# Passes over edges written out pair by pair, gather indices from one table in SBUF

## What is computed

```python
# layer 0: two convolutions with edge features (32), maximum over incoming edges
msg = x[src] @ W_msg + edge_attr_32 @ W_edge
agg = segment_max(msg, dst)                       # -inf -> 0
c   = leaky_relu(agg + x @ W_root + b)            # twice: c1, c2
# layer 1: edge features (17) through a small network, times the source's features, sum
w   = relu(edge_attr_17 @ W1.T + b1) @ W2.T + b2
agg = segment_sum(w * x[src], dst)
y   = relu(x @ Ws.T + bs + agg @ Wn.T + bn)
# layer 2: two hops h = segment_sum(norm[:, None] * h[src], dst), norm from the degrees
# layer 3: segment_sum((x * outdeg**-0.5)[src], dst) @ weight * indeg**-0.5 + bias
# after each layer: x = layernorm(x + layer(x))
```

## Time and profile before

| | before |
|---|---|
| median of three runs | 5490.79 us |
| the profiled execution | 5478.03 us, span 5476.3 us |
| granted TensorE clock, mean | 0.782 |
| PE / PEld busy | 73% / 48% |
| DVE busy | 41% |
| ACT busy | 18% |
| POOL busy | 47% |
| DMA, mean | 127 GB/s |

### The profile page before, as it was taken

One profiled execution on the slowest core, in us unless ns is written; L12 is line 12 of the kernel. 1 busy time (PEld: TensorE's weight loads), 2 busy tenths in 40 slices (PEclk: granted clock), 3 DMA queues, 4 the chain that ended last, 5 costly groups with the idle time before them and its releaser, 6 DMA issues.

```text
span 5476.3 us, 68119 instructions
## 1 busy us (share of the span) xinstructions
PE 3970.6 (73%) x19316; PEld 2615.8 (48%) x19316; DVE 2233.3 (41%) x5877; ACT 998.9 (18%) x2108; POOL 2583.1 (47%) x2689
## 2 busy tenths in 40 slices
PE   5766666676556667676746777766768668999999
PEld 4333333333423333333333444444444447999999
DVE  3544444454134444444433444344444344223211
ACT  1000000001112222222231222222222232001111
POOL 4566666664566666666645554545455541000000
PEclk9999999999965666666555666666665658999999
DMA  4333333333233444444422333333333334777776
GB/s 128 96 90 91 95 91 91 90 93 79 58 115 114 119 126 118 127 131 120 125 73 73 105 92 103 96 102 99 107 93 108 92 115 169 267 268 269 263 262 220
DMA packets 284287, 694.21 MB, mean 127 GB/s; under 512 B 105982, under 2 KB 188606, under 8 KB 260414
## 3 DMA queue, kind: packets, MB, share of 16 engines
q1 hardware_dynamic: 89090, 349.50, 19.1%
q0 software_dynamic: 85568, 131.83, 11.9%
q10 hardware_dynamic: 109564, 212.08, 10.5%
HBM read 479.08 MB, written 214.09 MB: 127 GB/s over the span
## 4 chain that ended last, share of the span: by engine, by line
PE 47%; another core or an unknown queue 28%; issue 12%; DVE 8%; ACT 2%; DVEq 1%; POOL 1%; DMA 1%; ACTq 0%; POOLq 0%; SPq 0%
PE banks L1099 16%; PE banks L963 8%; PE banks L1004 6%; PE banks L959 5%; PE banks L977 4%; PE banks L939 4%; PE banks L930 3%; DVE hot_lo L1465 2%; DVE hot_hi L1467 1%; DVE hot_key L1829 1%; DVE scan L1812 1%; DVE hot_src L1831 1%; POOL agg L635 1%; ACT adj L1332 1%
## 5 line engine op out<-in xcount | busy, mean ns | idle before, releaser
L692 POOL DMA_INDIRECT gath<-table,src_ix x2496 | 2406.4, 964 | 1778.5 <-issue 777.2
L1812 DVE TENSOR_TENSOR_SCAN scan<-keep,scan,banks 96x512 f32<-96x512 bf16 x621 | 791.3, 1274 | 1948.4 <-remote 1274.2
L1099 PE MATMUL banks<-r_parts,adj_in 128*128 128x288 bf16 x7203 | 890.0, 286 | 5.4 <-DVE r_parts L1513 2.7
L1099 PEld LDWEIGHTS banks<-r_parts,adj_in 128*128 128x128 bf16 x7203 | 883.1, 142 | 7.6 <-DVE r_parts L1513 3.5
L1004 PE MATMUL banks<-hot_key,hot_src 128*128 128x392 bf16 x1600 | 524.0, 461 | 451.7 <-issue 254.0
L977 PEld LDWEIGHTS banks<-ident,scan 96*128 96x128 f32 x2496 | 397.5, 223 | 901.5 <-issue 573.7
L963 PE MATMUL banks<-ea,w_edge 32*96 32x512 f32 x832 | 759.9, 1003 | 74.7 <-issue 73.3
L977 PE MATMUL banks<-ident,scan 96*128 96x96 f32 x2496 | 523.9, 356 | 320.0 <-DVE scan L1812 222.1
L1314 ACT ACTIVATE back<-banks 128x384 f32<-128x384 f32 x624 | 304.9, 491 | 2470.2 <-remote 1403.9
L1829 DVE TENSOR_SCALAR hot_key<-iota_key,key_t 128x392 bf16<-128x392 int16 x1600 | 507.9, 317 | 20.8 <-ACT key_t L1353 20.8
L939 PEld LDWEIGHTS banks<-w_edge_out,hid 97*128 97x128 f32 x1664 | 307.6, 277 | 436.7 <-issue 382.9
(11 more groups left out here) (158 smaller groups left out, 1998.5 us busy)
## 6 DMA issues: line engine op xcount, KB each, us to landing
adj_in<-adjacency SPq DMA_DIRECT2D x147, 1568.0 KB
scanned_rows<-back ACTq DMA_DIRECT2D x153, 768.0 KB
adjacency<-adj ACTq DMA_DIRECT2D x100, 784.0 KB
ea<-in_ea_t SPq DMA_DIRECT2D x156, 256.0 KB
gath<-table,src_ix POOLq DMA_INDIRECT x2496
keep<-keep_max_d SPq DMA_DIRECT2D x104, 384.0 KB
keep<-keep_sum_d SPq DMA_DIRECT2D x52, 384.0 KB
src_ix<-in_src_t SPq DMA_DIRECT2D x156, 8.0 KB
```

What stands on the lines that cost most here:

```text
L692: pool.indirect_dma_start(gath[:, b, t, :], None, tables[p][:, :], bass.IndirectOffsetOnAxis(ap=src_ix[:, b, t:t + 1], axis=0),).then_inc( ...
L1099: m = pe.matmul(sum_ps[:, u, j, :], adj_in[:, a, :, h], r_parts[:, n % 2, h, :, :].rearrange("p k f -> p (k f)"), start=h == 0, stop=h == ...
L1812: ve.tensor_tensor_scan(scan[0:D, b, at:at + Q], keep[:, b, at:at + Q], turn_ps[k % 2], start, keep_op, take_op).then_inc(s_scan, 1)
```

## The change

The loops `over_pairs` of the `Else` branch are replaced, on all five engines, by `all_pairs`, which issues all 26 pairs with known numbers. The `src_ix` loads, SP's waits for the gathers ahead of them and POOL's wait for them are gone: the gathers take their indices from `ids[:, 1, :]`, for which POOL waits once. A condition on ACT that told the first pair of pass 1 by its index being a number now tells it by the number. The general branch keeps its loops.

```diff
+        def all_pairs(pair, after_first=None):
+
+            for i in range(PAIRS):
+                pair(i, i == 0, i == PAIRS - 1)
+                if i == 0 and after_first:
+                    after_first()
...
@@ SP, loads_of_pair @@
-                            tiles = bass.ds(CT * (2 * i + b), CT)
-                            if not first:
-                                for k in range(4):
-                                    sp.wait_ge(s_gath[4 * b + k], 16 * QT * (PAIRS * p + i))
-                                sp.sem_inc(s_passed, 1)
-                            sp.dma_start(src_ix[:, b, :], src_t[:, tiles]).then_inc(s_ix[b], 16)
...
-                    over_pairs(sp, loads_of_pair)
+                    all_pairs(loads_of_pair)
...
@@ POOL @@
             with pool.Else():
+                pool.wait_ge(s_ids, 32)
...
-                            pool.wait_ge(s_ix[b], 16 * (PAIRS * p + i + 1))
...
+                                    n = CT * (2 * i + b) + t
                                     pool.indirect_dma_start(
                                         gath[:, b, t, :], None, tables[p][:, :],
-                                        bass.IndirectOffsetOnAxis(ap=src_ix[:, b, t:t + 1], axis=0),
+                                        bass.IndirectOffsetOnAxis(ap=ids[:, 1, n:n + 1], axis=0),
                                     ).then_inc(s_gath[4 * b + k], 16)
...
-                    over_pairs(pool, gather_pair)
+                    all_pairs(gather_pair)
...
-                    over_pairs(pe, pair, turn_lines if p == 0 else None)
+                    all_pairs(pair, turn_lines if p == 0 else None)
...
-                            if k % 4 == 0 and j == 0 and not (p == 1 and type(i) is int):
+                            if k % 4 == 0 and j == 0 and not (p == 1 and under(i, 0, 1)):
                                 act.wait_ge(s_adj[half], 16 * tile)
...
-                    over_pairs(act, pair, leave_lines if p == 0 else None)
+                    all_pairs(pair, leave_lines if p == 0 else None)
...
-                    over_pairs(ve, pair, make_keys if p == 0 else None)
+                    all_pairs(pair, make_keys if p == 0 else None)
```

## The result

The changed kernel takes 5193.18 us in the median of four runs (5168.95 to 5204.43), the kernel before 5490.2; the ratio is 0.946, with a 95% interval of 0.942 to 0.950. That is 297 us, twice the 145 that the prediction gave, though inside its range.

The account below looks back on a forecast made before the run. Bound: the consumers' work plus freezes, semaphores arriving late behind GpSimd's long runs of gathers. Gains of 35 + 20 + 80 + 1 = 136 us from 5478.0 gave 5342, stated as 5345; range 5150 to 5500.

Parts of the forecast that it names:

- B: Rival, all passes: without index stops, gather runs and freezes get longer, so the kernel is slower, 5655 us; chance 0.12.
- D: Rival, written-out code: it stalls some engine, 5634 us, or the change does nothing it says; chance 0.03.
- C: Rival, pass 2: runs break up, freezes shrink, TensorE's clock falls less; chunk 24.5 us instead of 30.1, 5152 us; chance 0.18.
- A: Rival, all passes: index stops are a result, not a cause, so nothing changes, 5478 to 5490 us; chance 0.17.
- The index part: Index loads and waits gone in the three edge passes: gains of 35, 20 and 80 us, plus 1 at the start.
- The 35 us of pass 0: Pass 0: 22 index stops shrink from 5.3 to 3.7 us, runs staying at four quarters; bounds 0 and 117 us.
- pass 2's 80 us: Pass 2: runs go from four quarters to three, 7.4 to 6.9 us a quarter, gaining 80 to 100 us, 80 taken.
- a floor of 6.85 us a quarter: Pass 2: runs of two quarters give at best 13.7 us for two, bounding the gain at 114 us.
- n*r + F: Edge passes: cycle of n quarters, consumers' time r each, plus freeze F = 5.0n + 2.7 - a; 24.8 us in pass 0.
- The loops: Loops written out on five engines, three passes: no gain, 0 us.
- the bound of 22 us: Loops written out: at most 72 back edges x 0.3 us, the pause before a gather, gained.
- the indices come 1.8 us later: Pass 0: ring-ended stops cost 3.74 us, index-ended 5.57; the ring is free at the thaw, indices land 1.8 us later.

Follow-up runs that it names:

- e15: Changed kernel with GpSimd waiting after every second quarter (8 gathers) until its own gathers have landed: 5232.42 us, 0.955 of the kernel before.
- e14: Changed kernel with only GpSimd's pass written out, indices from the table, the other four engines keeping their loops: 5223.12 us, 0.953 of the kernel before.
- e13: Kernel before with all five engines' loops written out, index loads and the waits on them kept: 5376.22 us against 5483.2, ratio 0.982.
- e17: Kernel before with SyncE's passes alone written out, index loads and all waits kept: 5399.35 us beside 5465.38, ratio 0.987.
- e11: Kernel before with TensorE turning every quarter three times instead of once: 5553.69 us beside 5473.22, ratio 1.016.
- e2: Changed kernel with index loads and their waits put back, all five engines written out: 4424.76 us beside 4429.01, ratio 0.999.
- e8: All five engines written out, index loads and waits kept, in the second set: 4428.1 us beside a kernel before of 4431.11.
- e9: All five engines written out, index loads and waits kept, in the third set: 4425.12 us against 4426.23 for the kernel before.
- e18: Changed kernel with a fill of an unused tile on GpSimd after every second quarter, without waiting for gathers: 5064.97 us, 0.926 of the kernel before.

## Why the prediction was right and wrong

**The direction and the mechanism.** Semaphores that are late behind long runs of gathers, stops for the indices that come out of it, runs of 12 in place of 16 in pass 2: this is what the traces show, and e15 shows that long runs of gathers make the lateness, since a wait for their landing after 8 takes it away. Rivals B and D did not come. Of C, pass 2 went more than half the way (26.8 us a chunk from 30.5, to C's 24.5): its runs broke up and its stops became short, as C says, but the granted clock stayed at 0.61, and did not rise. C's 5152 us lie nearer to the measured 5193 than the forecast's 5345. A, nothing changes, is what on-time sets give, for a reason that it did not have.

**The index part: forecast 35 + 20 + 80.** e14, which is this part with GpSimd's loop gone as well, has 32, 20 and 212 us. The 35 us of pass 0 rest on runs that stay at four quarters with stops of 3.7 us. The full change has just that (48 of 53 runs, 3.7 us). In e14 the number is as good, but by luck: 42 of its 79 runs are of three quarters, with shorter stops. The term that made the prediction wrong is pass 2's 80 us, where 185 came. It is a difference of two cycles, and both were mis-sized.

- The cycle before. I took 29.5 us a chunk from the one run of the earlier trace rows. The mean over the pass, without its first chunk, is 30.47, and the 33 runs of 16 have 31.04; the earlier trace rows itself gave 30.1. Over 50 chunks this is worth 48 us.
- The cycle after. The new cycle of three quarters was good, 20.8 us forecast and 20.4 measured. But I let every run have three quarters, and put a floor of 6.85 us a quarter under shorter ones ("n = 2 gives at best 10 + 3.7 = 13.7"). There were runs of 8 gathers at 12.0 us in the changed kernel (7 times) and at 12.7 in e14 (62 times), 6.0 and 6.4 us a quarter. My own formula gives 2 x 3.7 + (10 + 2.7 - 8) = 12.1 for them; the floor contradicted it. The mean came to 26.76 us a chunk where 20.8 x 4/3 = 27.7 was forecast, worth another 49 us.

The few us left are the rounding of 92 to 80 and of 52 chunks to 50. Together it is (30.47 - 26.76) x 50 = 185. The same counted at the stops: the pauses ahead of the gathers in pass 2 fell from 497.7 + 252.9 + 26.1 = 777 us to 335.7 + 245.6 + 13.4 = 595, by 182.

**The formula behind it.** The cycle n*r + F fits much of pass 2: without index loads runs of 8 gathers take 12.0 and 12.7 us and runs of 12 20.4 and 21.1 us from start to start (changed kernel and e14), where it gives 12.1 and 20.8; with them runs of 16 take 29.9 to 31.0 us (e13, e17, the kernel before), where it gives 29.5. But the 11 runs of 12 that the kernel before has there take 17.3 us. It does not describe pass 0, where it was fitted to runs of 16 alone: from 12 gathers to 16 it adds 9.0 us, the kernel before adds 7.3 (17.29 to 24.55), e14 6.2 (17.31 to 23.51) and the changed kernel 5.5 (17.88 to 23.40). Put to the runs that e14 has in pass 0 it gives 1121 us, and 1238 were measured. So what sets the length of a stop in pass 0 stays open. e11, which might have tested the formula, changed TensorE's clock as well and does not.

**The loops: forecast 0.** Wrong as a price: alone they bring 107 us (e13), since in the late time SyncE takes 0.7 us for an instruction and four stand between a `keep` and the index load, two of them for the loop's register alone. I had priced a back edge by the pause before a gather, 0.3 us, and by quarters 4.02 us apart in and out of the loop, all read from engines and moments that are not late; so the bound of 22 us was no bound. In the sum it mattered little: beside the index part they are worth some 30 us at most (5223 against 5193). The sentence "the indices come 1.8 us later" was right, and what made them late was to a good part SyncE's loop, which I named nowhere. The Trainium skill ("Runtime: NRT & Kernel Launch", Instruction fetch mechanics) favours full unrolling, against which I held the 33 + 32 packets. Unrolling did pay, but not by that rule: the kernel before fetched no more than that, and in on-time sets e2, e8 and e9 gain 0.1% at most.

**Small steps.** The start (first gather at 38.91 us, forecast 1 us earlier, 2 came), the dense stage (902.4 us from its first matmul to its last, before and after), no new idle "issue" of TensorE (its share of the chain fell from 12% to 6%): as forecast. The quarters of pass 0 stay 4.02 us apart in the late trace. The granted clock of 1.00 that the prediction reads in pass 0 is a stretch without a record; as r was read from the rows, the sum does not hang on it.

**What no step had.** That the whole effect belongs to one of two conditions of the machine. In the other the change is worth 0.2% (4420.84 against 4431.11 us), and the kernel before is 19% faster than the one that I read. Nothing in the one profile could say so, but the 28% of "another core or an unknown queue" on a single core was the place to ask.

## What to carry to other kernels

A cost on a queue has to be priced at the moment when the queue runs: the same wait or register instruction of SyncE was 0.08 us in one trace and 0.7 in the other, and it is the loads issued just then that the others wait for. When a difference is taken between a cycle before and a cycle after, take the mean of all rows for the one before, never one example, and hold every floor that you set against your own formula. When an edit is to make an engine slower, look at its busy time and its clock before reading anything from the pass's time. And where waits end by nothing that the profile can name, run the unchanged kernel again in other sets before explaining its time; a pause in a long run of gathers (e15, e18) is a cheap probe.

## What the runs showed of the hardware that I had not expected

- The same kernel takes 4426 to 4431 us or 5465 to 5490 us (medians of sets), on one and the same chip as well, and the runs of one set keep to one of the two. In the slower condition semaphores of the engines are late behind runs of 12 and 16 gathers (15 and 20 us); in the other not even behind 832 gathers in a row.
- In the late time SyncE steps at 0.7 or 1.4 us an instruction, and TensorE's matmuls have pauses of 1.1 us between them in which it waits for nothing that the profile shows.
- Three times the transposes made TensorE's quarters shorter where the clock rose with them: 3.21 us at a granted 1.00 against 4.02 us of the kernel before in pass 0, at the lower level.
- A wait of 2.4 us for the landing of its own gathers, after every 8, removes it (67 us of late waits ahead of the scan in place of 1232), a fill of 0.76 us on GpSimd does not (917).
- With half the gathers TensorE has no pauses (565 of 570 us busy in pass 1) and is granted a clock of 1.00, where it was 0.62 and busy for 865 of 1272 us: the pass takes 570 us there and 1272 beside late semaphores.
